# Turning the tokens of three half-stages on VectorE in 32x32 blocks and moving the blocks by DMA, in place of PE transposes

## The reference, cut to what matters

```python
x = x + tanh(g_xattn) * xattn(layernorm(x), ctx_1024, Wq, Wk, Wv, Wo, gq, gk)    # 16 heads of 128, q and k rms-normed
x = x + tanh(g_ffn) * ffn(layernorm(x), ln1_w, ln2_w, wq, wk, wv, wo, gate_w, ...)

def ffn(x):                       # x here is the layernormed input
    h = rmsnorm(x, ln1_w)         # h = x * rsqrt(mean(x^2) + eps) * ln1_w
    x = x + causal_attention(h)   # 16 heads of 128
    h = rmsnorm(x, ln2_w)
    top 6 of 16 experts by softmax(h @ gate_w.T), weights renormalised
    out = x + routed_experts(h) + shared_expert(h)
```

## Time and profile before

| | us |
|---|---|
| runs | 627.66, 628.72, 630.34 |
| the profiled execution's own time | 627.96 |
| its span in the trace | 626.1 |
| PE busy | 617.8 (99%) |
| PE weight loads busy | 526.1 (84%) |
| VectorE (DVE) busy | 461.7 (74%) |
| ScalarE (ACT) busy | 320.2 (51%) |
| GpSimd (POOL) busy | 254.0 (41%) |

### The profile page before, as it was taken

One profiled execution on the slowest core, in us unless ns is written; L12 is line 12 of the kernel. 1 busy time (PEld: TensorE's weight loads), 2 busy tenths in 40 slices (PEclk: granted clock), 3 DMA queues, 4 the chain that ended last, 5 costly groups with the idle time before them and its releaser, 6 DMA issues.

```text
span 626.1 us, 17387 instructions
## 1 busy us (share of the span) xinstructions
PE 617.8 (99%) x6906; PEld 526.1 (84%) x6906; DVE 461.7 (74%) x934; ACT 320.2 (51%) x699; POOL 254.0 (41%) x336
## 2 busy tenths in 40 slices
PE   8999999999999999999999999999999999999997
PEld 6788888888889888999999889988878788888885
DVE  5979787997886886786677899567566976575554
ACT  6867677777743334243434333454476444444442
POOL 3221211313144334344343354345545665455552
PEclk9999999999999999999999999999999999999999
DMA  7532130111021322222231321123344333334442
GB/s 232 189 89 67 52 103 28 41 39 37 18 70 48 106 69 69 70 68 78 66 115 40 115 70 36 35 64 96 95 99 109 81 102 101 89 95 104 104 119 81
DMA packets 45757, 51.42 MB, mean 82 GB/s; under 512 B 12784, under 2 KB 32752, under 8 KB 45680
## 3 DMA queue, kind: packets, MB, share of 16 engines
q1 hardware_dynamic: 44976, 49.86, 27.8%
q10 hardware_dynamic: 704, 0.48, 0.2%
HBM read 48.22 MB, written 1.05 MB: 79 GB/s over the span
## 4 chain that ended last, share of the span: by engine, by line
PE 93%; ACT 3%; DVE 2%; issue 1%; DMA 1%; SPq 0%; DVEq 0%; ACTq 0%
PE bank_q L564 16%; PE acc L591 14%; PE bank_k L564 14%; PE acc L626 10%; PE bank_v L564 8%; PE bank_s L564 7%; PE bank_v L687 7%; PE bank_k L767 2%; PE bank_s L735 2%; PE bank_p L784 2%; PE bank_s L745 2%; PE bank_p L718 1%; PE bank_t L752 1%; PE bank_q L708 1%; PE bank_k L697 1%
## 5 line engine op out<-in xcount | busy, mean ns | idle before, releaser
L1720 POOL TENSOR_TENSOR wq_lo<-raw_a,wq_hi 128x256 fp32r<-128x256 f32 x32 | 23.5, 735 | 115.8 <-DVE wq_hi L1491 115.8
L1720 POOL TENSOR_TENSOR wq_lo<-raw_m,wq_hi 128x256 fp32r<-128x256 f32 x50 | 42.0, 840 | 60.9 <-DVE wq_hi L1510 59.5
L1554 DVE TENSOR_TENSOR pv_lo<-raw_a,pv_hi 128x512 fp32r<-128x512 f32 (+1 forms) x51 | 38.3, 753 | 30.8 <-ACT pv_hi L1135 30.2
L1135 ACT ACTIVATE pv_hi<-raw_a 128x512 fp32r<-128x512 f32 (+1 forms) x51 | 31.7, 623 | 55.4 <-DVE raw_a L1549 53.8
L564 PE MATMUL bank_q<-xt_hi,wq_hi 128*128 128x512 f32 x144 | 59.8, 416 | 0.0
L564 PE MATMUL bank_q<-xt_hi,wq_lo 128*128 128x512 f32 x144 | 56.8, 394 | 0.0
L564 PE MATMUL bank_q<-xt_lo,wq_hi 128*128 128x512 f32 x144 | 56.5, 393 | 0.0
L1541 DVE TENSOR_TENSOR r_k<-ln_k,unit_w 128x512 f32<-128x512 f32 x44 | 30.6, 696 | 32.1 <-ACT ln_k L1126 31.9
L1720 POOL TENSOR_TENSOR wk_lo<-raw_m,wk_hi 128x256 fp32r<-128x256 f32 x50 | 37.6, 753 | 30.5 <-ACT wk_hi L1210 30.5
L1720 POOL TENSOR_TENSOR wv_lo<-raw_v,wv_hi 128x512 fp32r<-128x512 f32 x16 | 20.7, 1294 | 67.9 <-DVE wv_hi L1517 67.9
L1720 POOL TENSOR_TENSOR wo_lo<-raw_m,wo_hi 128x256 fp32r<-128x256 f32 x50 | 41.5, 830 | 7.2 <-ACT wo_hi L1204 7.2
(11 more groups left out here) (254 smaller groups left out, 2097.3 us busy)
## 6 DMA issues: line engine op xcount, KB each, us to landing
raw_m<-in_chunk_m SPq DMA_DIRECT2D x50, 256.0 KB, 2.8
raw_a<-in_head_a SPq DMA_DIRECT2D x48, 192.0 KB, 3.1
raw_b<-in_head_b SPq DMA_DIRECT2D x32, 256.0 KB, 3.1
raw_m<-in_chunk_m SPq DMA_DIRECT2D x50, 128.0 KB, 2.1
raw_v<-in_pair_v SPq DMA_DIRECT2D x16, 256.0 KB, 2.9
raw_b<-in_head_b SPq DMA_DIRECT2D x32, 128.0 KB, 2.1
vs<-qt SPq DMA_DIRECT2D x32, 32.0 KB, 2.0
xs<-in_x SPq DMA_DIRECT2D x6, 128.0 KB, 3.3
```

Source lines behind the costliest of these rows:

```text
L1135: nc.scalar.activation(pv_hi[:, u.parity, part], hh[:, part], ACT.Copy).then_inc(M["hh_hi"], 1)
L1554: nc.vector.tensor_tensor(pv_lo[:, u.parity, part], hh[:, part], pv_hi[:, u.parity, part], ALU.subtract)\
L1720: nc.gpsimd.tensor_tensor(lo, raw, hi, ALU.subtract).then_inc(signal, 1)
```

## The change

Three of the six turns, those of ("x", 1), ("y", 0) and ("y", 1), are made in another way. VectorE transposes `hn` in 32x32 blocks into a new tile `blocks` (two instructions of 128x512). SyncE moves each group of blocks to its partitions with 16 DMAs of 32 KB into `xt`, which holds nothing else at that time. ScalarE then copies from `xt` into `xt_hi`, and GpSimd subtracts into `xt_lo`. The turns of ("x", 0), ("t", 0) and ("t", 1) stay on PE.

The pieces have new places: `blocks` is VectorE's part, `split` is ScalarE's and GpSimd's. The pieces before them move to earlier pairs. For step "y" the weights `ln1_w` were a scale per partition after the turn; now they must be applied before it, along the free axis, so `scale` multiplies by a row of weights (`SM_LNROW`, 256 more columns in the constants) with `scalar_tensor_tensor`.

```diff
-    beside_pairs("a", 0, ("x", 1), stats=(pairs - 5, 2), norm=(pairs - 4, 2), turn=(pairs - 3, 0))
-    beside_pairs("a", 1, ("y", 0), stats=(1, 2), rough=(1, 1), norm=(2, 2), sums=(3, 0), root=(3, 1), scale=(4, 2),
-                 turn=(5, 0))
-    beside_pairs("b", 0, ("y", 1), stats=(1, 1), norm=(2, 1), sums=(3, 0), root=(3, 1), scale=(4, 1), turn=(5, 0))
+    beside_pairs("a", 0, ("x", 1), stats=(pairs - 7, 2), norm=(pairs - 6, 2), blocks=(pairs - 5, 0),
+                 split=(pairs - 2, 0))
+    beside_pairs("a", 1, ("y", 0), stats=(1, 2), rough=(1, 1), norm=(2, 2), sums=(2, 0), root=(2, 1), scale=(3, 2),
+                 blocks=(4, 0), split=(6, 0))
+    beside_pairs("b", 0, ("y", 1), stats=(1, 1), norm=(2, 1), sums=(3, 0), root=(3, 1), scale=(4, 0), blocks=(4, 1),
+                 split=(6, 0))
...
+        blocks = sb("blocks", [P, NT * D])
+        turned_x = xt[:].rearrange("p k n -> p (k n)")
...
+        MOVED = {("x", 1): 1, ("y", 0): 2, ("y", 1): 3}
+        TURNED = {("x", 0): 0, ("t", 0): 1, ("t", 1): 2}
...
         def key_sums(u):
-            turned = u.n > 1 and plan.piece(u.prev())[0] == "turn"
-            return (bank_v if turned else bank_p)[:, 0:HT // 2]
+            return bank_p[:, 0:HT // 2]
...
+            def move_blocks(step, to=range(QUADS)):
+                sp.wait_ge(blocks_ready, MOVED[step])
+                sp.wait_ge(ctxt_lo_ready, HALVES)
+                sp.wait_ge(xt_lo_ready, KD * PREP[step])
+                for m in to:
+                    found = blocks[:].rearrange("p (b m r) -> p b m r", m=QUADS, r=GROUP)[:, :, m, :]
+                    place = turned_x[m * GROUP:(m + 1) * GROUP].rearrange("c (b a r) -> c b a r", a=QUADS, r=GROUP)
+                    for a in range(QUADS):
+                        sp.dma_start(place[:, :, a, :], found[a * GROUP:(a + 1) * GROUP]).then_inc(ld_blocks, 16)
...
                 if n + 2 < HALVES * PAIRS:
                     reload_a1(n + 2)
+                if n in (4, 5):
+                    move_blocks(("x", 1), range(2 * n - 8, 2 * n - 6))
+                if n == PAIRS + 5:
+                    move_blocks(("y", 0))
...
                 if n + 1 < HALVES * PAIRS:
                     reload_b1(n + 1)
+                if n == 6:
+                    move_blocks(("y", 1))
...
+                if piece == "split":
+                    act_e.wait_ge(ld_blocks, 16 * QUADS * QUADS * MOVED[step])
+                    for k in range(KD):
+                        nc.scalar.activation(by_chunk(xt_hi[step[1]][:, k, :]), chunk_of(k), ACT.Copy).then_inc(xt_hi_ready, 1)
...
                 if piece in ("scale", "apply"):
-                    v.wait_ge(pe_tr, KD * PREP[step])
+                    if kind == "y":
+                        v.wait_ge(ld_rest, 16)
                     for t in range(NT):
-                        last = nc.vector.tensor_scalar(hn[:, t, :], ys[:, half, t, :], st[:, 2, t:t + 1], None, ALU.mult)
-                    last.then_inc(tok_ready, 1)
+                        if kind == "y":
+                            weights = sm[:, SM_LNROW:SM_LNROW + D]
+                            dve.mark(nc.vector.scalar_tensor_tensor(hn[:, t, :], ys[:, half, t, :], st[:, 2, t:t + 1], weights,
+                                                                    ALU.mult, ALU.mult))
+                        else:
+                            v.wait_ge(pe_tr, KD * TURNED[step])
+                            last = nc.vector.tensor_scalar(hn[:, t, :], ys[:, half, t, :], st[:, 2, t:t + 1], None, ALU.mult)
+                    if kind == "t":
+                        last.then_inc(tok_ready, 1)
+                if piece == "blocks":
+                    v.wait_ge(dve.sem, dve.n)
+                    if MOVED[step] > 1:
+                        v.wait_ge(ld_blocks, 16 * QUADS * QUADS * (MOVED[step] - 1))
+                    for t in range(0, NT, 2):
+                        last = nc.vector.transpose(blocks[:, t * D:(t + 2) * D], hn[:, t:t + 2, :].rearrange("p t d -> p (t d)"))
+                    last.then_inc(blocks_ready, 1)
...
+            def prepare(u):
+                piece, step = piece_at(u)
+                if piece == "split":
+                    for k in range(KD):
+                        pool.wait_ge(xt_hi_ready, KD * PREP[step] + k + 1)
+                        rest(by_chunk(xt_lo[step[1]][:, k, :]), chunk_of(k), by_chunk(xt_hi[step[1]][:, k, :]), xt_lo_ready)
...
                 for h in range(2):
                     split_head(after, h)
+                    if not h:
+                        prepare(u)
...
                 for h in range(2):
                     split_out(u, h)
+                prepare(u)
                 if nxt.kind == "b":
                     split_head(after, 1)
```

More of the change, by code:

```diff
@@ L229, in flamingo_layer @@
     SM_TIE = SM_MASK + SEQ
-    SM_W = SM_TIE + E * E
+    SM_LNROW = SM_TIE + E * E
+    SM_W = SM_LNROW + D
     with ExitStack() as stack:
@@ L347, in flamingo_layer @@
         pe_cw = sem("pe_cw")
+        blocks_ready, ld_blocks = sem("blocks_ready"), sem("ld_blocks")
         tok_ready, first_tokens = sem("tok_ready"), sem("first_tokens")
@@ L788, in turn_tokens @@
             def turn_tokens(step, banks):
-                pe.wait_ge(tok_ready, PREP[step])
+                pe.wait_ge(tok_ready, TURNED[step])
                 for k, bank in enumerate(banks):
@@ L825, in prepare @@
                 return []
-            def turned_tokens(u):
-                piece, step = piece_at(u)
-                return [(xt_lo_ready, KD * (PREP[step] + 1))] if piece == "turn" else []
             def release(held):
@@ L998, in take_tokens @@
                 for k, bank in enumerate(banks):
-                    act_e.wait_ge(pe_tr, KD * PREP[step] + k + 1)
+                    act_e.wait_ge(pe_tr, KD * TURNED[step] + k + 1)
                     def take(target):
@@ L1003, in take @@
                             return nc.scalar.activation(target[:, k, :], bank[:], ACT.Copy)
-                        col = (SM_LN1 if kind == "y" else SM_LN2) + k
+                        col = SM_LN2 + k
                         return nc.scalar.activation(target[:, k, :], bank[:], ACT.Identity, scale=sm[:, col:col + 1])
                     if kind == "t" and not half:
+                        act_e.wait_ge(xt_lo_ready, KD * PREP[step])
                         last = take(xt)
@@ L1319, in prepare_piece @@
                             last.then_inc(first_tokens, 1)
-                    if PREP[step]:
-                        last.then_inc(tok_ready, 1)
+                        else:
+                            dve.mark(last)
                 if piece == "norm" and kind != "x":
@@ L1641, in self_pair @@
                     read_acc(prev)
-                early = piece_at(u)[0] in ("turn", "logits")
+                early = piece_at(u)[0] in ("turn", "blocks", "logits")
                 if early:
@@ L1862, in lay_out @@
         a["L0_xattn_gq"].reshape(P, 1), a["L0_xattn_gk"].reshape(P, 1),
-        a["L0_ffn_ln1_w"].reshape(K, P).T, a["L0_ffn_ln2_w"].reshape(K, P).T,
+        a["L0_ffn_ln2_w"].reshape(K, P).T,
         np.broadcast_to(a["g_xattn"].reshape(1, 1), (P, 1)), np.broadcast_to(a["g_ffn"].reshape(1, 1), (P, 1)),
         a["L0_ffn_gate_w"].T.reshape(K, P, E).transpose(1, 0, 2).reshape(P, K * E),
-        np.eye(P, dtype=f), mask, np.broadcast_to(tie, (P, E * E))], axis=1)
+        np.eye(P, dtype=f), mask, np.broadcast_to(tie, (P, E * E)),
+        np.broadcast_to(a["L0_ffn_ln1_w"].reshape(1, -1), (P, D))], axis=1)
     ctx_pairs = ctx.reshape(HALVES, 2, 4, 2, SEQ // 2, C).transpose(2, 4, 0, 1, 3, 5).reshape(P, -1)
```

12 lines of the change are left out of this document (8 added, 4 removed).

## The result

The changed kernel took 630.43 us in the median of 20 executions (628.99 to 632.41), the kernel before 628.75 in 20 on the same chips. The ratio is 1.0024 (95%: 1.0017 to 1.0032), so +1.1 to +2.0 us where -0.5 was forecast. The profiled execution took 628.99 us with a span of 626.8, against 627.96 and 626.1 before. The time is in the range of 625.4 to 631.4 and within 0.5% of before; the forecast and its direction were wrong.

The account below looks back on a forecast made before the run. PE, busy 99% of the span, was taken to bound the kernel. -2.64 (turns) - 0.87 (old wait) + 2.24 (new wait) + 0.75 (GpSimd) = -0.52 us, forecasting 628.2 against a median of 628.72; range 625.4 to 631.4 us.

Parts of the forecast that it names:

- the four terms of the sum: PE's removed turns, returned wait, new wait and GpSimd wait: -2.64 - 0.87 + 2.24 + 0.75 = -0.52 us.
- The turns: Three turns off PE, in cross half 0, cross half 1 and self half 0: 2.64 us less.
- The old wait: Pair 3 of cross half 1: PE's wait behind (y,0)'s squares on ScalarE goes, 0.87 us come back.
- The new wait: Pair 2 of cross half 1: squares wait for VectorE's norm, PE waits 2.24 us for the query copy.
- The subtractions on GpSimd: For (y,0), pair 6 of cross half 1: PE's first queries of self half 0 wait 0.75 us.
- The moves of (y,0): Rival, pair 6 of cross half 1: DMAs land late for ScalarE's split, 629.5 to 632.7 us; chance 0.11.
- the statistics of (x,1) in pair 1: Cross half 0: VectorE's earlier statistics cost nothing, within an end above of 0.3 us for the VectorE additions.
- the GpSimd subtraction of (x,1): Cross half 0: both subtractions done by 91.3, PE's queries start at 92.52; costs nothing, end above 0.3 us.
- The scaling: VectorE, pair 3 of cross half 1: weights along the free axis add 0.3 us, costing nothing, end above 0.3.
- VectorE late: Rival: transposes, costlier scaling and GpSimd beside VectorE delay the scores, 629.6 to 630.6 us; VectorE or GpSimd late: 0.19.
- any wait that PE is given costs its full length: Premise for PE, busy 99% at clock 1.00: a wait costs its length, so 2.24 us costs 2.24.
- the clean gain: Rival: the new waits on PE do not appear, 3.5 us come off, 625.2 us; clean or mostly clean: 0.20.

Follow-up runs that it names:

- Experiment 7: The kernel before with one unread 128x512 GpSimd subtraction added in each of twelve cross-stage pairs: 630.49 us, 1.0034.
- experiment 6: The changed kernel with statistics, norm and blocks of (x,1) one pair later and its 16 moves together: 630.75 us, 1.0027.
- experiment 8: The changed kernel with the edits of experiment 4, experiment 5 and experiment 6 together: 626.86 us, 0.9971 of the kernel before.
- experiment 13: The changed kernel with the edits of experiment 4 and experiment 6, and the turn of (y,0) back on PE: 628.16 us, 0.9988.
- experiment 14: The changed kernel with the edits of experiment 4 and experiment 6, all three turns moved: 627.62 us, 0.9980.
- experiment 15: The same edits as experiment 8 on the changed kernel, run again on another chip: 627.04 us, 0.9969.
- experiment 16: The kernel before with only the turn of (x,1) moved, its statistics, norm and blocks a pair later, moves together: 628.18 us, 0.9990.
- experiment 5: The changed kernel with GpSimd making the tokens' low parts ahead of both heads of weights in the cross stages: 631.10 us, 1.0039.
- only (y,0): The changed kernel with only the turn of (y,0) made with blocks and moves, the other two back on PE: 631.56 us, 1.0048.
- experiment 9: The kernel before, all turns on PE, with only (y,0)'s sum of squares and root moved to pair 2 of cross half 1: 630.30 us, 1.0014.
- experiment 10: The changed kernel with seven 128x512 zero products on PE, one pair too early for the long wait: 633.29 us, 1.0069.
- experiment 11: The changed kernel with seven 128x512 zero products on PE directly ahead of the 2.2 us wait: 631.30 us, 1.0038.
- experiment 4: The changed kernel with step y's mean squares worked out from variance and root on VectorE, no squares on ScalarE: 628.17 us, 0.9988.

## Why the prediction was wrong

**Right: the four terms of the sum.** The turns: -0.87, -0.91, -0.87 by the offsets, where 0.88, 0.90 and 0.86 were written. The old wait came back with 1.04 instead of 0.87. The new wait was 2.18 for 2.24, by the mechanism given. The subtractions on GpSimd were 0.74 for 0.75. The moves of (y,0) did not land late, although the sixteen took 0.71 us each on average, at the 0.72 from which that rival was to decide; one issue of 1.54 us made the difference to 0.61. They had landed at 170.0, and ScalarE came for them at 172.48, not at the 170.30 assumed. The 170.30 had the removed turn's 0.90 taken off, but not the prediction's other terms ahead of it (-0.88, -0.87 and +2.24), by which it would have been 170.8; PE was in fact 1.4 us later there than before. So the room was 2.5 us where 1.8 were written: the outcome was right, the time in it was not.

**Wrong: two terms put at nothing, the statistics of (x,1) in pair 1 (under "Added on VectorE") and the GpSimd subtraction of (x,1) ("Both cost nothing").** This is a loss of 0.71 + 0.46 us, and its mechanism was not in the list. The statistics in pair 1 push the weight rounding from 31.03 to 33.50, GpSimd's subtractions follow it, and one of them now runs while VectorE makes the sum of squares. DVE, POOL and PE after, where pair 1 of cross half 0 passes into pair 2:

```profile
33.50 0.46 DVE L1535 CAST wq_hi<-raw_a 128x256 fp32r<-128x256 f32 x2
...
34.95 0.73 POOL L1764 TENSOR_TENSOR wq_lo<-raw_a,wq_hi 128x256 fp32r<-128x256 f32 x1
34.95 0.75 DVE L1453 TENSOR_TENSOR ssq<-sums_t,eps_q 128x8 f32<-128x8 f32 x1
35.62 0.68 DVE L1476 TENSOR_TENSOR sc_sub<-bank_s,r_k 128x512 f32<-128x512 f32 x1
...
36.35 0.50 PE L594 MATMUL bank_s<-ctxt_hi,wk_hi 128*128 128x512 f32 x1 [0.52 <-DVE sc_sub L1476]
```

The same place before:

```profile
33.15 0.46 POOL L1720 TENSOR_TENSOR wk_lo<-raw_a,wk_hi 128x128 fp32r<-128x128 f32 x1
...
34.31 0.17 DVE L1409 TENSOR_TENSOR ssq<-sums_t,eps_q 128x8 f32<-128x8 f32 x1
```

A sum of 8 numbers a row takes 0.75 us and ends at 35.70, where GpSimd's subtraction ends at 35.68. PE waits for what stands behind it. At the start of pair 7 it is the new subtraction of the tokens. DVE and POOL after:

```profile
88.77 2.52 POOL L1764 TENSOR_TENSOR xt_lo<-xt,xt_hi 128x512 fp32r<-128x512 f32 x2
90.62 0.69 DVE L1453 TENSOR_TENSOR ssq<-sums_t,eps_q 128x8 f32<-128x8 f32 x1
```

Again both end together, at 91.29 and 91.31. PE's idle time there is only 0.1 us; the rest of the +0.46 shows as later starts at the next keys and at the first output, not as a wait. The prediction did write that this subtraction is early enough for PE, which it is. It did not ask who else is held while it runs. Experiment 7 shows that GpSimd's work alone can have such a price, experiments 6, 8 and 13 to 16 that the 0.71 goes with the statistics' place. The 0.46 went in experiment 5, but experiments 8 and 15, with the same order of GpSimd's work, have 0.29 and 0.33 there. In experiment 8 the sum, 0.74 us long, meets a subtraction of weights in its place, and both end at 90.9. So the order moved the meeting rather than ended it.

The Trainium skill (SBUF — State Buffer, "SBUF: two separate sides") describes a port pair that one of VectorE and GpSimd holds alone for a whole instruction while the other waits, also when VectorE's operation has two inputs in SBUF and GpSimd's reads SBUF. The ends that coincide, here and in experiment 7, agree with it.

**Wrong: the scaling at 0.3 us and no consequence.** Four operations took 480 ns each against 350 before, +0.5 us. The line after (ns min/median/max, first and last start):

```profile
L1368 DVE SCALAR_TENSOR_TENSOR hn<-ys,st,sm x8: 478/480/486, 141.4 to 257.8; 128x256 f32<-128x256 f32 x8
```

The prediction's estimate of 0.5 from the Trainium skill (VectorE: DVE Perf Modes, "Mode 2×_2P — use both read ports for one tensor") was the better figure. The scaling now stands in pair 3, ahead of that pair's rounding of weights, VectorE does not idle from there to the scores of pair 4, and PE waits for it: the step of +0.60. DVE and PE after, pair 4:

```profile
146.41 0.68 DVE L1476 TENSOR_TENSOR sc_sub<-bank_s,r_k 128x512 f32<-128x512 f32 x1
...
147.15 0.50 PE L594 MATMUL bank_s<-ctxt_hi,wk_hi 128*128 128x512 f32 x1 [0.26 <-DVE sc_sub L1476]
147.20 0.92 DVE L1481 TENSOR_TENSOR sc<-sc_sub,r_q 128x512 f32<-128x512 f32 x1
...
154.03 1.29 DVE L1380 STREAM_TRANSPOSE blocks<-hn 128x512 f32<-128x512 f32 x2
```

This is the rival "VectorE late" in small. The block transposes of (y,0) start at 154.03, behind the loss, so they did not make it. PE loses about half of it here, with its wait of 0.26 us, and the other half at the first output 3 us later, behind an operation on the scores that takes 0.92 us instead of 0.69. Experiment 13, which moves the scaling back with the turn, has no such step. No run parted the scaling's price from its place.

**Wrong: "any wait that PE is given costs its full length", so 2.24 us for a wait of 2.24 us.** It has a second price, a fall of TensorE's granted clock behind it, in part of the executions. Counted at a mean clock of 0.997 or less: the changed kernel 8 of 20, only (y,0) 5 of 6, experiment 5 4 of 5, experiment 6 8 of 12, experiment 9 3 of 12, experiment 10 4 of 6. All have the 2.2 us wait. In the eleven other experiments, whose longest wait is 1.5 us, at the kernel's start, it is none of 114 executions. The first windows of 1 us behind the wait in experiment 5's trace:

```profile
133.00:134.00 1.00, 0.59 (x12) 0.88 0.00 0
134.00:135.00 1.00, 1.00 (x21) 0.50 0.21 32
...
137.00:138.00 1.00, 1.00 (x33) 0.91 0.05 16
```

and in the profiled execution of the changed kernel, which had the wait but not the fall:

```profile
133.00:134.00 1.00, 0.65 (x13) 1.00 0.00 0
134.00:135.00 1.00, 1.00 (x65) 1.00 0.30 49
```

65 matmuls in the second microsecond against 21. Experiment 9 shows that the wait is enough, without any of the moves. Experiment 11, with the same delay, PE busy for most of it and no fall, speaks for PE's idling as the cause, on a chip on which the fall itself was never seen.

**Of the rivals** the clean gain did not come. The slower one with the late moves did not either. What came was a piece of "VectorE late" and two mechanisms that no rival priced: that rival does have "GpSimd's longer use beside it", but no place and no time for it. The slower side had 0.30 of the chance and lay at 629.5 or above.

## What to carry to other kernels

Price a new wait on a saturated TensorE twice: its length, and what the clock does behind it; a profile in which the clock held proves nothing about the next execution, so count the executions by their granted clock. Before work is moved in time on VectorE, lay GpSimd's instructions beside the short two-input operations on the path, since an operation of 0.17 us can last as long as the one it meets. And when moving a piece makes a wait, look for another source of the same number: here the variance that VectorE already held did away with the squares, and with their wait, in the kernel before too.

## What the runs showed of the hardware

- TensorE's granted clock fell to 0.50 for about 3.4 us, from 0.4 to 1.1 us after the end of an idle time of 2.17 us, in some executions of the same program and not in others. The price was 1.3 us in one trace, and 1.5 us between the medians of the changed kernel's executions.
- Stalls with no releaser at the 64-column matmuls of the self stages: PE idled 0.2 us at them in the profiled execution of before, 0.3 after, 1.0 in experiment 13, 1.8 in experiment 11. Two executions of one program (experiments 8 and 15) had steps in the self stages in the same pairs with other lengths (+0.06 and +0.31, +0.23 and +0.29, +0.14 and +0.25). Such steps move a kernel by 1 us and more, as much as a turn, and no experiment found their cause.
- The experts' stage, which the change does not touch before its own two pieces, ran 227.1 us behind the last pair's scores in the changed kernel, against 228.1 in before. Other kernels with all three moves had 227.1 to 227.7 and those with none 227.4 to 227.9, so how much of it is the change's is open.
- Moves of 32 KB took 0.61 us of SyncE's queue in the median, in rows of 16 as in twos, with single ones of 1.2 to 1.7 us among them: 11.43 us for the 16 of (y,0).
- The fastest version is the change with experiments 4, 5 and 6: 626.86 and 627.04 us, 0.9971 (0.9960 to 0.9982) and 0.9969 (0.9959 to 0.9979) of the kernel before.
